# Mamba-2 mixer in a decoder kernel: norm weights applied to the activations, and twelve lower weight parts made by GpSimd

## The reference, cut to what matters

```
residual = hidden_states
h = rmsnorm(hidden_states, norm_w)
zxbcdt = jnp.einsum('bld,ed->ble', h, in_proj_w)
z, xBC, dt = jnp.split(zxbcdt, ...)
xBC = silu(causal depthwise conv of width 4 over xBC, + conv_b)
x, Bm, Cm = jnp.split(xBC, ...)
dt = softplus(dt + dt_bias); dA = exp(dt * A)
h_t = h_{t-1} * dA_t + dt_t * B_t * x_t ;  y_t = h_t . C_t     (scan over tokens)
y = rmsnorm((y + D * x) * silu(z), ssm_norm_w)
h = residual + jnp.einsum('ble,de->bld', y, out_proj_w)
```

## Time and profile before

| | us |
|---|---|
| time, median of 3 runs (lowest, highest) | 2704.47 (2703.77, 2705.28) |
| the profiled execution, its own time | 2701.48 |
| its span | 2699.7 |
| PE busy in it | 2660.4 |
| DVE, ACT, POOL busy in it | 1481.7, 1039.0, 707.9 |
| mean granted clock of PE, as a share of full | 0.998 |

### The profile page before, as it was taken

The page is one execution under the profiler, slowest core; times in us unless marked ns, Lnnn a source line. Parts: engine busy times, 40 slices in busy tenths (PEclk is TensorE's granted clock), DMA queues, the critical chain, the costliest instruction groups (busy, mean ns, idle before and its releaser), DMA issues.

```text
span 2699.7 us, 42475 instructions
## 1 busy us (share of the span) xinstructions
PE 2660.4 (99%) x15264; PEld 2071.1 (77%) x15264; DVE 1481.7 (55%) x2533; ACT 1039.0 (38%) x2403; POOL 707.9 (26%) x622
## 2 busy tenths in 40 slices
PE   7999999999999999999999999999999999999999
PEld 5777777777778888888888867777777767777776
DVE  8787787787785321332233277777777773111122
ACT  6434435434434222122212155555555553222221
POOL 5653653563561100010100111332133321000000
PEclk9999999999999999999999999999999999999999
DMA  4011001101114101110111221110111123211111
GB/s 155 10 39 47 25 22 47 46 0 47 47 48 142 63 1 62 62 62 0 62 62 46 72 72 50 63 62 8 62 62 54 58 87 133 78 47 47 47 47 47
DMA packets 85482, 147.83 MB, mean 55 GB/s; under 512 B 4032, under 2 KB 17984, under 8 KB 85408
## 3 DMA queue, kind: packets, MB, share of 16 engines
q1 hardware_dynamic: 85408, 146.84, 15.7%
HBM read 113.27 MB, written 33.55 MB: 54 GB/s over the span
## 4 chain that ended last, share of the span: by engine, by line
PE 84%; issue 9%; DVE 4%; DMA 2%; ACT 1%; POOL 1%; POOLq 0%; DVEq 0%; ACTq 0%
PE ps L75 20%; PE ps L77 20%; PE ps L76 20%; PE ps L1860 5%; PE ps L2223 4%; PE ps L855 3%; PE ps L1872 2%; PE ps L1851 2%; PE ps L830 1%; PE ps L843 1%; DVE mx_cv L628 1%; PE ps L785 1%; DMA gm_r<-h_scratch 1%; DMA x_scratch<-gm_r 1%; PE ps L1803 1%
## 5 line engine op out<-in xcount | busy, mean ns | idle before, releaser
L1553 ACT ACTIVATE at_pr<-ps,at_nm 128x256 f32<-128x256 f32 x512 | 235.5, 472 | 181.7 <-DVE at_nm L1707 181.7
L1229 DVE TENSOR_TENSOR gm_m_lo<-gm_m,gm_m_hi 128x512 fp32r<-128x512 f32 (+1 forms) x88 | 60.9, 692 | 417.1 <-ACT gm_m_hi L1146 417.1
L75 PE MATMUL ps<-sh_u_hi,gm_gu_hi 128*128 128x512 f32 (+1 forms) x704 | 274.7, 390 | 0.0
L76 PE MATMUL ps<-sh_u_lo,gm_gu_hi 128*128 128x512 f32 (+1 forms) x704 | 274.6, 390 | 0.0
L77 PE MATMUL ps<-sh_u_hi,gm_gu_lo 128*128 128x512 f32 (+1 forms) x704 | 274.6, 390 | 0.0
L1140 ACT ACTIVATE gm_sg<-ps 128x512 f32<-128x512 f32 (+1 forms) x88 | 52.7, 598 | 517.7 <-PE ps L77 517.6
L1713 DVE COPY at_pT<-ps 128x512 f32<-128x512 f32 x256 | 176.0, 688 | 125.4 <-PE ps L1860 122.2
L564 POOL TENSOR_TENSOR mx_m<-mx_m,mx_g 128x512 f32<-128x512 f32 x128 | 164.8, 1288 | 244.9 <-DVE mx_m L641 244.8
L75 PE MATMUL ps<-sh_u_hi,qm_w_hi 128*128 128x512 f32 x512 | 201.5, 393 | 0.2 <-DVE qm_w_lo L225 0.2
L77 PE MATMUL ps<-sh_u_hi,qm_w_lo 128*128 128x512 f32 x512 | 199.4, 389 | 0.0
L76 PE MATMUL ps<-sh_u_lo,qm_w_hi 128*128 128x512 f32 x512 | 199.2, 389 | 0.0
(11 more groups left out here) (255 smaller groups left out, 6358.6 us busy)
## 6 DMA issues: line engine op xcount, KB each, us to landing
sh_xf<-x_scratch SPq DMA_DIRECT2D x16, 1024.0 KB, 7.3
mx_xr<-in_x SPq DMA_DIRECT2D x8, 1024.0 KB, 5.9
h_scratch<-mx_xr SPq DMA_DIRECT2D x8, 1024.0 KB, 5.1
sh_xf<-h_scratch SPq DMA_DIRECT2D x8, 1024.0 KB, 8.0
gm_xr<-in_x SPq DMA_DIRECT2D x8, 1024.0 KB, 7.2
gm_r<-h_scratch SPq DMA_DIRECT2D x8, 1024.0 KB, 6.1
x_scratch<-gm_r SPq DMA_DIRECT2D x8, 1024.0 KB, 5.1
at_cf<-in_ctxT SPq DMA_DIRECT2D x16, 512.0 KB, 4.2
```

The source lines that it names most:

```text
L75: nc.tensor.matmul(out, l_hi, r_hi, start=first, stop=False)
L76: nc.tensor.matmul(out, l_hi, r_lo, start=False, stop=False)
L1553: A(pr[h][:, t, :], SC[h][:, SEQ * t:SEQ * t + SEQ], ACT.Exp, bias=nm[:, 4 * n + h, t:t + 1], accum_out=sums[:, 2 * b + t, 4 * g + h:4 * g ...
```

## The change

The weights are no longer scaled: all pieces have `None` as their scale. Instead the norm weights scale the activations as these are split. `u_hi` is made with `scale=norm_w` and `u_lo` by one `scalar_tensor_tensor` (value times weight minus `hi`) instead of a `tensor_tensor`; `g_hi` and `g_lo` likewise with `ssm_w`. The split for the stage behind (`ahead(i - 1)`) stays as it was. Upper parts of all 28 pieces are made by ACT. POOL makes the lower parts of the last twelve (pieces 16 to 27), with one subtraction each, and begins them when `dal` is done, not when the first piece lands. On ACT, two upper parts move ahead of the exponential of the decays, and the following ones each by one conv tile; DVE makes the lower part of piece 15 ahead of `daT` and has none behind that.

```
@@ Weights
-            if p["by_pool"]:
-                continue
             act.wait_ge(self.su.load[p["slot"]], p["loaded"])
...
         for p in self.pieces[self.pool_next:upto]:
-            pool.wait_ge(self.su.load[p["slot"]], p["loaded"])
-            G.tensor_scalar(p["staged"], p["staged"], p["scale"], None, ALU.mult).then_inc(self.su.pool_scaled, 1)
-            pool.wait_ge(self.su.pool_scaled, p["scaled"])
-            G.tensor_copy(p["hi"], p["staged"]).then_inc(self.su.pool_hi, 1)
             pool.wait_ge(*p["hi_at"])
             G.tensor_tensor(p["lo"], p["staged"], p["hi"].bitcast(F32), ALU.subtract).then_inc(self.su.pool_lo, 1)
@@ stage_mixer
-            pieces.append((wi[k][:, o:e], hi[:, k, at_e], lo[:, k, at_e], norm_w[:, k:k + 1]))
+            pieces.append((wi[k][:, o:e], hi[:, k, at_e], lo[:, k, at_e], None))
...
-        pieces.append((wo[k], wout_hi[:, k, :], wout_lo[:, k, :], ssm_w[:, k:k + 1]))
+        pieces.append((wo[k], wout_hi[:, k, :], wout_lo[:, k, :], None))
...
-    wt = Weights(nc, su, places, pieces, lambda n: n if n < IN_PIECES else IN_PIECES + n % TT, IN_PIECES)
+    wt = Weights(nc, su, places, pieces, lambda n: n if n < IN_PIECES else IN_PIECES + n % TT, IN_PIECES - KD)
@@ scalar
-            A(u_hi[:, k, :], turned(i, k)[:, :], ACT.Copy).then_inc(s["uhi"], 1)
+            kind = {} if ahead(i - 1) else {"scale": norm_w[:, k:k + 1]}
+            A(u_hi[:, k, :], turned(i, k)[:, :], ACT.Copy, **kind).then_inc(s["uhi"], 1)
...
             tap(i, 1)
+            if step_0(i):
+                wt.high(act, 3 * KD + 2)
...
-                    wt.high(act, min(3 * KD + 2 * (n - 1), IN_PIECES))
+                    wt.high(act, 3 * KD + 2 * n)
...
-                A(g_hi[j % 2][:, :], zs[j % 2][:, :], ACT.Copy).then_inc(s["gs"], 1)
+                A(g_hi[j % 2][:, :], zs[j % 2][:, :], ACT.Copy, scale=ssm_w[:, j:j + 1]).then_inc(s["gs"], 1)
@@ gpsimd
-                pool.wait_ge(su.small, smalls)
+                pool.wait_ge(s["dal"], 1)
                 wt.by_pool(pool, len(pieces))
@@ vector
+            if ahead(i - 1):
+                V.tensor_tensor(u_lo[:, k, :], src, hi, ALU.subtract).then_inc(s["ulo"], 1)
+            else:
+                V.scalar_tensor_tensor(u_lo[:, k, :], src, norm_w[:, k:k + 1], hi, ALU.mult, ALU.subtract).then_inc(s["ulo"], 1)
...
+            V.scalar_tensor_tensor(g_lo[j % 2][:, :], zs[j % 2][:, :], ssm_w[:, j:j + 1], g_hi[j % 2][:, :].bitcast(F32),
+                                   ALU.mult, ALU.subtract).then_inc(s["glo"], 1)
...
                     wt.low(dve, 3 * KD + n - 1)
+            if step_0(i):
+                wt.low(dve, 4 * KD)
             dve.wait_ge(s["dat"], i + 1)
...
-                if step_0(i):
-                    wt.low(dve, 3 * KD + n - 1)
-            if step_0(i):
-                wt.low(dve, IN_PIECES)
```

More of the change, by code:

```diff
@@ L85, in __init__ @@
         self.small, self.hi, self.lo = sem("set_small"), sem("set_hi"), sem("set_lo")
-        self.pool_scaled, self.pool_hi, self.pool_lo = sem("set_pool_scaled"), sem("set_pool_hi"), sem("set_pool_lo")
+        self.pool_lo = sem("set_pool_lo")
         self.pool_pieces = 0
@@ L171, in __init__ @@
                 su.pool_pieces += 1
-                p["scaled"], p["hi_at"], p["lo_at"] = su.pool_pieces, (su.pool_hi, su.pool_pieces), (su.pool_lo, su.pool_pieces)
+                p["lo_at"] = su.pool_lo, su.pool_pieces
             else:
-                su.his += 1
                 su.los += lo is not None
-                p["hi_at"], p["lo_at"] = (su.hi, su.his), (su.lo, su.los)
+                p["lo_at"] = su.lo, su.los
+            su.his += 1
+            p["hi_at"] = su.hi, su.his
             cols = 1
@@ L588, in split @@
             dve.wait_ge(s["uhi"], KD * i + k + 1)
-            V.tensor_tensor(u_lo[:, k, :], turned(i, k)[:, :], u_hi[:, k, :].bitcast(F32), ALU.subtract).then_inc(s["ulo"], 1)
+            src, hi = turned(i, k)[:, :], u_hi[:, k, :].bitcast(F32)
+            if ahead(i - 1):
+                V.tensor_tensor(u_lo[:, k, :], src, hi, ALU.subtract).then_inc(s["ulo"], 1)
+            else:
+                V.scalar_tensor_tensor(u_lo[:, k, :], src, norm_w[:, k:k + 1], hi, ALU.mult, ALU.subtract).then_inc(s["ulo"], 1)
         def first(i):
@@ L655, in g_low @@
             at(dve, s["out"], KI * i + j - 1)
-            V.tensor_tensor(g_lo[j % 2][:, :], zs[j % 2][:, :], g_hi[j % 2][:, :].bitcast(F32),
-                            ALU.subtract).then_inc(s["glo"], 1)
+            V.scalar_tensor_tensor(g_lo[j % 2][:, :], zs[j % 2][:, :], ssm_w[:, j:j + 1], g_hi[j % 2][:, :].bitcast(F32),
+                                   ALU.mult, ALU.subtract).then_inc(s["glo"], 1)
         def dt_first(i):
```

## The result

The changed kernel takes 2709.6 us in the median of 15 runs (2706.05 to 2712.0); the kernel before takes 2703.9 in the 15 runs beside it (2699.99 to 2705.83). The ratio is 1.0023, with an interval of 1.0016 to 1.003: slower by 5.7 us in the medians, and by 4.3 to 8.1 by the interval. The forecast was 2708.7, or 4.2 us more than before. The text had taken 0.2% as what can be told from nothing; the measured 0.23% lies about on that bound.

What follows compares the result with a forecast made beforehand. The prediction took PE's queue as the bound, with the change touching only the mixer's step 0. Terms -0.4 + 1.3 + 3.9 + 1.3 - 1.9 sum to +4.2 us, 2704.5 to 2708.7 us, range 2703.5 to 2711.3.

Steps and rivals of the forecast that it cites:

- term 2: Behind PE's longer wait at `spread(0)`: a second slow-clock stretch, +1.3 us (0 to 2.6).
- term 4: Behind PE's wait of about 4.4 us at `chunk_y(0)`: the slow clock again, +1.3 us (0 to 2.6).
- The decays: Step 0's start: `dta` and `dal` fall to 0.23 us, clock stays up, PE 3.2 us earlier at `conv_in(4)`.
- Term 1: At `spread(0)`, waiting for DVE: `daT` comes only 0.4 us earlier, so -0.4 us (-1.1 to 0).
- rival B: Each of the two slow stretches lasts twice as long as today's: +6.8 us, 2711.3 us; chance 0.12.
- Term 3: At `chunk_y(0)`: POOL's last two subtractions, held by ACT's upper parts, delay the first products, +3.9 us (3.5 to 4.5).
- Term 5: Between chunks 1 and 2: PE's wait for DVE goes, -1.9 us (-1.9 to -1.0).
- The activations: Every step: longer scaled copies and subtractions on ACT and DVE cost 0, at most 0.1 us for each of 7 steps.
- Rival C: Longer activation copies and subtractions reach PE in each step: 2.8 us on top, 2711.5 us; chance 0.05.
- Rival D: POOL is ready in time, terms 3 and 4 are gone: 2703.5 to 2702.2 us; chance 0.10.
- rival E: GpSimd's own speed on the twelve subtractions bounds: +7.2 us, 2711.7 us; chance 0.03.
- rival A: The clock falls once only, or not at all: 2707.4 us, or 2706.1 with neither; chance 0.25.

Runs made afterwards that it cites:

- experiment 11: Changed kernel with only ACT's upper parts of pieces 12 and 13 moved back behind the exponential of the decays: 2707.8 us, ratio 1.0019.
- experiment 4: Changed kernel with POOL beginning its twelve subtractions when `daT` is copied instead of when `dal` is done: 2704.3 us, ratio 1.0011.
- Experiment 2: Changed kernel with 16 filler matmuls ahead of `spread(0)` and 16 ahead of `chunk_y(0)` in step 0: 2705.0 us, ratio 1.001.
- experiment 3: Kernel before with only the scaling moved to the activations; POOL still makes both parts of pieces 20 to 27: 2704.6 us, ratio 1.001.
- experiment 1: Changed kernel with POOL's last two subtractions (pieces 26 and 27) behind the products of heads 0 and 1: 2702.2 us, ratio 0.9998.
- experiment 6: Changed kernel with `daT` copied behind the first conv tile and the last two subtractions behind the products of heads 0 and 1: 2700.0 us, ratio 0.999.
- experiment 10: Kernel of experiment 9 with ACT's upper parts of pieces 12 and 13 back behind the exponential: 2699.4 us, ratio 0.9984.
- experiment 5: Changed kernel with `daT` copied behind the first conv tile in step 0: 2702.3 us, ratio 1.0000.
- experiment 7: Kernel before with `daT` copied behind the first conv tile in step 0: 2704.0 us, ratio 1.0006.
- experiment 9: Kernel of experiment 6 with DVE's scan of head 1 ahead of conv tile 7 in step 0: 2701.0 us, ratio 0.9992.

## Why the prediction was right

The direction, the two new waits and who releases them, the wait that is absorbed, and the steady steps came as forecast. The difference came out 1.5 us above the forecast, 5.7 instead of 4.2. In step 0 the terms come to 6.0: term 2 was mis-sized by 1.5 and term 4 by 0.3. That the medians also give 1.5 is in part luck, since the profile holds more that the sum did not have (last points below).

- **The decays: right.** `dta` and `dal` take 0.23 and 0.22 us (forecast 0.23), PE doesn't wait for `dal`, and the clock from 30 to 35 us is 1.00. PE gained and gave all of it back at `spread(0)`, as the text said.
- **Term 1, -0.4: measured -0.4, by two errors that cancel.** I had the two upper parts ahead of the exponential at nothing, and experiment 11 gives 1.04 us. Their cover was to be 2.38 us of idling less 1.1. But counted from dt's copy, `dta` ends 2.5 us earlier than before (at +8.5 us, not +11.1), and ahead of the exponential ACT also has a table load of 1.28 us, in both kernels; before, it was over when the idling of 2.38 us began. ACT's timeline of after has the two upper parts, that load and the exponential without a gap:

```profile
26.28 1.14 ACT L213 ACTIVATE mx_wz_hi<-mx_stage 128x512 fp32r<-128x512 f32 x2
27.44 1.28 ACT L487 ACT_TABLE_LOAD   x1
28.73 0.26 ACT L487 ACTIVATE mx_dt_da<-mx_dt_dta 128x64 f32<-128x64 f32 x1
```

  The exponential starts at +9.8 us; without the two upper parts (experiment 11) it starts at +8.7, right behind the load. So no cover was left. I had read two collisions with POOL, `dta` and `dal`; DVE's timeline of before has four more instructions in the same chain that take longer than in after, each beside POOL's scaling or copying of a piece:

```profile
21.60 0.38 DVE L664 SCALAR_TENSOR_TENSOR mx_dt_nab<-mx_dt_a 128x64 f32<-128x64 f32 x1
22.30 0.54 DVE L668 TENSOR_SCALAR mx_dt_u<-mx_dt_ee 128x64 f32<-128x64 f32 x1 [0.32 <-ACT mx_dt_ee L464]
22.88 0.67 DVE L670 SCALAR_TENSOR_TENSOR mx_dt_c<-mx_dt_u,mx_dt_ee 128x64 f32<-128x64 f32 x1
...
26.56 0.58 DVE L681 SCALAR_TENSOR_TENSOR mx_dt_dt<-mx_dt_a,mx_dt_sp 128x64 f32<-128x64 f32 x1
```

  In after these four take 0.20 to 0.23 us: 1.3 us more won than in the sum, and about as much lost behind two upper parts on ACT. The first conv tile behind `dal` comes 1.7 us earlier, as forecast (1.5 to 1.6). The collision further on cost 1.0 to 1.1 us (experiment 4), not 0.7.
- **Term 2, +1.3: measured +2.8. This is the term that was mis-sized.** The distance from `spread(0)` to `spread(1)` is 5.89 and 5.86 us at full clock (experiments 2 and 3), and 7.17, 7.33 and 7.41 in experiments 1, 11 and 4: that is the 1.3 to 1.5 of my term, and their windows have some 3.4 us at 1.2 GHz, as before. In the changed kernel, both times, it is 8.67 and 8.65, with some 6.8 us at 1.2 GHz. The text had twice the usual length as the term's upper bound (2.6) and in rival B. The step that failed was taking the one slow stretch of before as the usual length. What sets the length stays open.
- **Term 3, +3.9: measured +4.6, less 0.7.** From `tap(8)` to `chunk_y(0)` are 7.88 us; the text's working (0.7, 0.63, two subtractions, 3.9) gives 61.7 - 53.84 = 7.9. Comparing with 57.82 of before hid a small wait in between: `spread(3)` waited for DVE's scans, as PE's timeline of before has it:

```profile
54.66 0.49 PE L843 MATMUL ps<-mx_daT,mx_sel 128*128 128x512 f32 x1 [0.42 <-DVE mx_m L641]
```

  By the marks that stretch is 0.7 us longer than in after. The wait is gone there, as PE comes later, and the hold is by so much longer. The difference of the two is the 3.9.
- **Term 4, +1.3: measured +1.6.** Experiment 2 shows for both terms that it is the clock: with the waits filled, 4.4 us go from step 0.
- **Term 5, -1.9: measured -1.9.** It does not come back in experiment 1, where PE is as early as before, and 1.38 us of it are there in experiment 3, where the lower parts of z are still DVE's. So it was these lower parts that made it, and PE's lateness did not merely hide it.
- **The activations, 0: measured 0.01 us per step** (99.32 against 99.31 in experiment 3, 99.33 in the changed kernel). Rival C wanted 0.35 us in each step, and falls by that; the median of experiment 3, some 2.7 us above before, is not explained.
- **Rival D** (POOL ready in time) falls by POOL's timeline, **rival E** by experiment 1, **rival A** by the windows: both clock falls came. **Rival B** came half: one of the two slow stretches lasted twice as long.
- **What the sum did not have:** dt's product at the head. Its groups of eight matmuls (L884) start 1.68 us apart in the profile of after, against 0.85 before, so dt's copy comes 1.5 us later. Of the profiles here, those of the changed kernel and of 1, 4, 6, 10 and 11 have the copy at 18.96 to 19.47 us, those of before and of 2, 3, 5, 7 and 9 at 17.40 to 17.98. Nothing was tried on that. The forecast of 0.1 us later was wrong for both executions, and whether it is in the medians is open.
- **And the mixer's last step.** PE waits there for ACT's `zsilu`, in every profile, for 1.7 to 2.0 us; PE's timeline of after:

```profile
782.08 0.66 PE L831 MATMUL ps<-sh_ident,mx_xc 128*128 128x128 f32 x4 [1.94 <-ACT mx_zs L452]
```

  In both profiles of the changed kernel a slow stretch follows (clock 0.79 and 0.87 from 780 to 790 us) and PE loses 1.6 us by it; before, with 1.74 us of waiting, the clock stays at 1.00. The same stretch is slow in experiments 4, 7 and 9 and at full clock in the others, so it goes with neither kernel. The 8.3 us between the two profiled executions are 1.5 at the head, 6.0 in step 0, some 2 up to the end of the mixer, and 1.4 less behind it.

## What to carry to other kernels

Work given to an idle engine costs by its place in that engine's queue and by who releases its last item, not by the engine's idle share or its speed: look for what others need from behind it. A wait taken away upstream is kept only if the next wait in line isn't on the same busy engine; here three such gains were given back at the next place. Before an idle stretch is used as cover, list all that it covers already, a table load included, and price a new wait of a few microseconds on TensorE at 1.3 to 2.8 us more than the wait itself, knowing that it can also be nothing; with harmless matmuls to fill the wait that surcharge goes, but not the wait.

## What the runs showed of the hardware

- **Clock.** Ahead of `spread(0)`, a wait of 4.5 us was followed by a loss of 2.8 us twice and of 1.3 us once; waits of 3.43 and 4.13 us by 1.5 and 1.4, waits of 4.5 us ahead of `chunk_y(0)` by 1.5 to 2.7 (`chunk_y(0)` to `spread(4)` 6.25 to 7.39 us against 4.72), one of 2.28 us by 1.6, and waits of `spread(3)` of 2.23 and 3.27 us (experiments 6 and 7) by 1.6 each; waits of 3.42, 2.75 and 2.54 us were followed by none. In the last step one and the same wait of 1.7 to 2.0 us was followed by a slow stretch in 5 of 13 profiles. A kernel with 32 matmuls more (ratio 1.001) is faster than the same one without them (1.0023 and 1.0025).
- **SBUF.** A DVE subtraction of 128x512 with both inputs in SBUF took 1.68 us beside two POOL subtractions and 0.68 otherwise, and 1.75 in experiment 10. It isn't only instructions with two inputs: in experiment 3 the one-input copy of `da` (L702) took 1.08 us beside a subtraction, where it takes 0.18 before and in after; and beside POOL instructions that read one tile only, the four dt instructions of before took 0.15 to 0.45 us longer than in after. So the prediction's rule, two inputs on both sides, is too narrow. The Trainium skill, "GPSIMD Engine Reference", section "Specifications", names this contention without a size; the rows give some 1.0 us for such a meeting, and 1.1 for an instruction of 0.23 us.
